# One block of a layer's down-projection: both halves of its tokens for each input block, and a wait for each block

## The reference, cut to what matters

```python
for i in range(4):
    residual = x
    q, k, v = x @ Wq[i] + bq[i], x @ Wk[i] + bk[i], x @ Wv[i] + bv[i]
    Q, K = elu(q) + 1, elu(k) + 1
    KV, Ksum = sum_over_tokens(K * v), sum_over_tokens(K)
    V = Q * KV / (Q * Ksum + 1e-6)
    a = gelu(gelu(V @ Wo[i] + bo[i]))
    x = ln(a + residual, ln1_s[i], ln1_b[i])
    residual = x
    h = gelu(x @ W1[i] + b1[i])          # 128 -> 512
    f = gelu(h @ W2[i] + b2[i])          # 512 -> 128, the down-projection
    x = ln(f + residual, ln2_s[i], ln2_b[i])
x = layernorm(x_in + x)
h = layernorm(gelu(x @ ternary(W_fc).T), ln_w, ln_b)
x = layernorm(x + h @ ternary(W_proj).T)
```

## Time and profile before

| | |
|---|---|
| time before, median of 3 runs | 479.62 us (478.72 to 481.2) |
| time of the profiled execution | 478.65 us |
| its span, first to last instruction | 476.5 us |
| granted TensorE clock, mean over the span | 0.982 |
| PE matmul busy | 442.0 us, 93%, 2074 records |
| DVE busy | 402.6 us, 85%, 1391 |
| ACT busy | 371.9 us, 78%, 483 |
| GpSimd (POOL) busy | 13.9 us, 3%, 19 |

### The profile page before, as it was taken

One profiled execution on the slowest core, in us unless ns is written; L12 is line 12 of the kernel. 1 busy time (PEld: TensorE's weight loads), 2 busy tenths in 40 slices (PEclk: granted clock), 3 DMA queues, 4 the chain that ended last, 5 costly groups with the idle time before them and its releaser, 6 DMA issues.

```text
span 476.5 us, 6527 instructions
## 1 busy us (share of the span) xinstructions
PE 442.0 (93%) x2074; PEld 309.2 (65%) x2074; DVE 402.6 (85%) x1391; ACT 371.9 (78%) x483; POOL 13.9 (3%) x19
## 2 busy tenths in 40 slices
PE   7697999999999999999999999999989999799992
PEld 6465665756575656566656665667566756688992
DVE  5988889995989698969896988698878897978897
ACT  3989877989897989798889888989888717778106
POOL 0000000000000000000000000000000003230000
PEclk9978999999999999999999999999999999999997
DMA  8200000000100000001000000000010102000003
GB/s 285 70 2 0 22 3 0 1 0 1 45 0 2 23 0 1 1 0 45 0 2 1 1 0 1 0 1 2 0 45 12 34 7 82 2 0 23 2 23 132
DMA packets 5360, 10.40 MB, mean 22 GB/s; under 512 B 848, under 2 KB 1872, under 8 KB 5328
## 3 DMA queue, kind: packets, MB, share of 16 engines
q1 hardware_dynamic: 5040, 9.47, 6.1%
q10 hardware_dynamic: 288, 0.52, 0.3%
HBM read 7.90 MB, written 2.10 MB: 21 GB/s over the span
## 4 chain that ended last, share of the span: by engine, by line
PE 41%; DVE 32%; ACT 19%; issue 7%; DMA 1%; ACTq 0%; SPq 0%; DVEq 0%
PE tile L1249 10%; PE tile L1268 7%; PE tile L1226 6%; PE tile L1222 6%; PE tile L1223 5%; DVE stats L770 5%; ACT y L369 3%; DVE y L911 3%; DVE nt L777 2%; ACT y L374 2%; PE tile L1339 2%; PE tile L1328 2%; ACT aa L388 2%; DVE y L880 2%; ACT kq L348 2%
## 5 line engine op out<-in xcount | busy, mean ns | idle before, releaser
L1249 PE MATMUL tile<-h,w 128*128 128x512 f32 x256 | 113.9, 595 | 0.9 <-ACT h L395 0.7
L1222 PE MATMUL tile<-xh,wh 128*128 128x512 f32 x224 | 97.6, 436 | 6.1 <-DVE xh L793 3.4
L1223 PE MATMUL tile<-xh,wl 128*128 128x512 f32 x224 | 89.2, 398 | 0.0
L1249 PEld LDWEIGHTS tile<-h,w 128*128 128x128 f32 x256 | 47.4, 190 | 54.8 <-issue 51.7
L395 ACT ACTIVATE h<-tile,vec 128x1024 f32<-128x1024 f32 x64 | 71.0, 1117 | 13.1 <-PE tile L1226 12.3
L1226 PE MATMUL tile<-xl,wh 128*128 128x512 f32 x224 | 71.1, 398 | 0.7 <-DVE xl L298 0.3
L403 ACT ACTIVATE nt<-tile,work 128x128 f32<-128x128 f32 x140 | 50.7, 482 | 11.3 <-DVE work L739 11.3
L1222 PEld LDWEIGHTS tile<-xh,wh 128*128 128x128 f32 x224 | 42.6, 190 | 24.9 <-DVE xh L793 5.3
L770 DVE BATCH_NORM_STATS2 stats<-tile 128x6 f32<-128x128 f32 x256 | 52.8, 280 | 0.1
L1226 PEld LDWEIGHTS tile<-xl,wh 128*128 128x128 f32 x224 | 41.6, 188 | 13.5 <-DVE xl L799 2.7
L1223 PEld LDWEIGHTS tile<-xh,wl 128*128 128x128 f32 x224 | 42.8, 191 | 9.1 <-issue 2.2
(11 more groups left out here) (173 smaller groups left out, 669.6 us busy)
## 6 DMA issues: line engine op xcount, KB each, us to landing
x<-x_t SPq DMA_DIRECT2D x7, 512.0 KB, 4.1
out_r<-x SPq DMA_DIRECT2D x8, 256.0 KB, 2.0
raw_u<-layers SPq DMA_DIRECT2D x4, 256.0 KB, 3.2
w<-layers SPq DMA_DIRECT2D x4, 256.0 KB, 3.3
raw_a<-layers SPq DMA_DIRECT2D x4, 192.0 KB, 2.8
x<-x_t ACTq DMA_DIRECT2D x2, 256.0 KB, 3.9
wo<-layers SPq DMA_DIRECT2D x4, 64.0 KB, 4.2
fc<-fc_t SPq DMA_DIRECT2D x1, 256.0 KB, 6.5
```

Of the source, the lines that this page charges most:

```text
L1222: pe.matmul(dst, wh[:, w0:w0 + P], xh[:, part(n, p, at)], start=True, stop=False)
L1223: pe.matmul(dst, wl[:, w0:w0 + P], xh[:, part(n, p, at)], start=False, stop=False)
L1249: mm = pe.matmul(dst, w2[:, (t - 1) // 2 % 2, j * P:(j + 1) * P], h[:, p, j * PAIR + at:j * PAIR + at + BANK], start=(j == 0), stop=(j == ...
```

## The change

`down(t, p, half, first)` becomes `down(t, p, j)`, which handles one block for both halves and waits for that block alone. Four calls take the place of two, and they always stand together, at the place where the first of the two calls stood; the calls that stood between the halves come after them.

```diff
-            def down(t, p, half, first):
-                if first:
+            def down(t, p, j):
+                if j == 0:
                     take(slot_of(t, "f", p), (f_ready[p], t))
-                    pe.wait_ge(h_ready[p], FT * t)
                     pe.wait_ge(w2_in[(t - 1) // 2 % 2], 16 * ((t - 1) // 4 + 1))
-                dst, at = halves(slot_of(t, "f", p))[half]
-                for j in range(FT):
+                pe.wait_ge(h_ready[p], FT * (t - 1) + j + 1)
+                for dst, at in halves(slot_of(t, "f", p)):
                     mm = pe.matmul(dst, w2[:, (t - 1) // 2 % 2, j * P:(j + 1) * P], h[:, p, j * PAIR + at:j * PAIR + at + BANK],
                                    start=(j == 0), stop=(j == FT - 1))
-                mm.then_inc(f_mm[p], 1)
+                    if j == FT - 1:
+                        mm.then_inc(f_mm[p], 1)
```

The four places where the order of the calls changes:

```diff
             fold_out(1)
-            down(1, 1, 0, True)
+            down(1, 1, 0)
+            down(1, 1, 1)
+            down(1, 1, 2)
+            down(1, 1, 3)
             attention_out(1, 0)
             back("1", 0, 0, 1)
             back("1", 0, 0, 0)
-            down(1, 1, 1, False)
             attention_out(1, 1)
...
             turned("1", 7, 0)
-            down(7, 0, 0, True)
+            down(7, 0, 0)
+            down(7, 0, 1)
+            down(7, 0, 2)
+            down(7, 0, 3)
             back("1", 7, 1, 0)
             back("1", 7, 1, 1)
-            down(7, 0, 1, False)
             back("1", 7, 0, 1)
...
-            down(8, 0, 0, True)
+            down(8, 0, 0)
+            down(8, 0, 1)
+            down(8, 0, 2)
+            down(8, 0, 3)
             turned("x", 0, 0)
-            down(8, 0, 1, False)
             back("x", 0, 1, 0)
-            down(8, 1, 0, True)
+            down(8, 1, 0)
+            down(8, 1, 1)
+            down(8, 1, 2)
+            down(8, 1, 3)
             back("x", 0, 1, 1)
             back("x", 0, 0, 1)
             back("x", 0, 0, 0)
-            down(8, 1, 1, False)
             turned("2", 8, 0)
```

```diff
             def final_sum(p, u):
                 n, q = p // 2, p % 2
                 dve.wait_ge(x_cb[p], 1)
+                if n == 0:
+                    dve.wait_ge(moment["g"][q], HIDDEN_STEPS)
+                else:
+                    dve.wait_ge(moment["x"][q], 3 * MOMENT_STEPS)
```

More of the change, by code:

```diff
@@ L674, in _, with chain @@
         def _(dve):
-            def norm_work(k, t, p, u=None):
-                pair, rows = home(k, t, p), slice(0, ROWS) if u is None else slice(u * HALF, (u + 1) * HALF)
+            def chain(k, t, p):
+                pair = home(k, t, p)
                 if k == "h":
[L680 to L683, removed]
@@ L685, in moments @@
-            def moments(*norms):
[L690 to L764, removed]
@@ new lines, in mean_square, with variance @@
+            def mean_square(k, t, p):
+                done, base, (rstd, shift, m, v, a, b), width = chain(k, t, p)
+                if k == "g":
+                    dve.wait_ge(done, base)
+                    dve.scalar_tensor_tensor(a, m, -1.0, m, ALU.mult, ALU.mult).then_inc(done, 1)
+                else:
+                    dve.wait_ge(done, base - 2)
+                    dve.scalar_tensor_tensor(a, a, width / 4.0, a, ALU.mult, ALU.mult).then_inc(done, 1)
+            def variance(k, t, p):
+                done, base, (rstd, shift, m, v, a, b), width = chain(k, t, p)
+                dve.wait_ge(done, base + 1)
+                if k == "g":
+                    dve.tensor_tensor(v, a, b, ALU.add).then_inc(done, 1)
+                else:
+                    dve.scalar_tensor_tensor(v, b, width * (BLOCK_EPS if k in "12" else OUTER_EPS), a, ALU.add,
+                                             ALU.add).then_inc(done, 1)
@@ new lines, in guess, with guess_squared @@
+            def guess(k, t, p):
+                done, base, (rstd, shift, m, v, a, b), width = chain(k, t, p)
+                dve.wait_ge(done, base + 2)
+                dve.tensor_scalar(b.bitcast(I32), v.bitcast(I32), -0.5, GUESS, ALU.mult, ALU.add).then_inc(done, 1)
+            def guess_squared(k, t, p):
+                done, base, (rstd, shift, m, v, a, b), width = chain(k, t, p)
+                dve.wait_ge(done, base + 3)
+                dve.tensor_tensor(a, b, b, ALU.mult).then_inc(done, 1)
@@ new lines, in near_one, with quadratics @@
+            def near_one(k, t, p):
+                done, base, (rstd, shift, m, v, a, b), width = chain(k, t, p)
+                dve.wait_ge(done, base + 4)
+                dve.scalar_tensor_tensor(a, a, (LEAD * width ** 0.5) ** 0.25, v, ALU.mult, ALU.mult).then_inc(done, 1)
+            def quadratics(k, t, p):
+                done, base, (rstd, shift, m, v, a, b), width = chain(k, t, p)
+                lead = (LEAD * width ** 0.5) ** 0.25
+                dve.wait_ge(done, base + 5)
+                dve.scalar_tensor_tensor(v, a, Q1 * lead, a, ALU.add, ALU.mult).then_inc(done, 1)
+                dve.scalar_tensor_tensor(shift, a, Q2 * lead, a, ALU.add, ALU.mult).then_inc(done, 1)
@@ new lines, in first_product, with root @@
+            def first_product(k, t, p):
+                done, base, (rstd, shift, m, v, a, b), width = chain(k, t, p)
+                dve.wait_ge(done, base + 6)
+                dve.scalar_tensor_tensor(b, v, C1 * (LEAD * width ** 0.5) ** 0.5, b, ALU.add, ALU.mult).then_inc(done, 1)
+            def root(k, t, p):
+                done, base, (rstd, shift, m, v, a, b), width = chain(k, t, p)
+                dve.wait_ge(done, base + 8)
+                dve.scalar_tensor_tensor(rstd, shift, C2 * (LEAD * width ** 0.5) ** 0.5, b, ALU.add, ALU.mult).then_inc(done, 1)
@@ new lines, in row_shift @@
+            def row_shift(k, t, p):
+                done, base, (rstd, shift, m, v, a, b), width = chain(k, t, p)
+                if k != "g":
+                    dve.wait_ge(done, base + 9)
+                    dve.scalar_tensor_tensor(shift, m, -0.5, rstd, ALU.mult, ALU.mult).then_inc(done, 1)
+            def moments(*norms):
+                for level in (sums, mean_square, variance, guess, guess_squared, near_one, quadratics, first_product, root,
+                              row_shift):
+                    for n in norms:
+                        level(*n)
@@ L1344, in projected, with warm_up @@
                     mm.then_inc(p_mm[p % 2], 1)
-            pe.wait_ge(const_ready, 7)
-            for _ in range(WARM_UP):
-                pe.matmul(tile[3][:, 0:P], ones[:, :], ones[:, :], start=True, stop=True)
+            def warm_up():
+                pe.wait_ge(const_ready, 7)
+                for _ in range(WARM_UP):
+                    pe.matmul(tile[3][:, 0:P], ones[:, :], ones[:, :], start=True, stop=True)
+            warm_up()
             attention_in("k", 0, 0)
```

93 lines of the change are left out of this document (70 added, 23 removed).

## The result

The changed kernel takes 487.93 us (median of 4 runs, 487.23 to 488.24) against 479.17 us before in the same job: ratio 1.0178, 95% interval 1.0162 to 1.0195, 8.8 us slower. Forecast were 488.3 us, in a range of 484.0 to 491.5. The profiled execution took 488.24 us, its span is 486.3; that is 9.8 more than the span of before, one microsecond more than the medians differ by.

What follows compares the result with a forecast made beforehand. No engine alone bounds the kernel; the chain passes between engines, so late starts matter. Profiled 478.65 + 3.44 + 2.25 + 2.2 + 0.8 = 487.35 us, against the median 488.3, range 484.0 to 491.5.

Steps and rivals of the forecast that it cites:

- The wait: Down-projection's finer wait on ACT's gelu: gain 0, at most 0.9 us, since `take` already waits for the last gelu.
- The inner order and the waits: Reordered matmuls: 0, kept -0.6 to +0.6 us; 48 added PE waits: taken as 0, at most 0.08 us each.
- Place A: Step 1, pair 1: `attention_out(1, 0)` and the backs move behind the second half; all engines run 3.44 us late.
- The idle of 2.8 and 1.1 us: Sign at Place A: PE idle for about 2.8 and 1.1 us between 64.6 and 69.4.
- Place B: Step 7: pair 1's two backs move behind the second half, delaying `gelu_down`, `second_sum` and `outer_sum(1)`: +2.25 us.
- Place C: Step 8: pair 1's transposes move behind the second half, delaying `outer_high`, `outer_low` and `second_sum(8, 1)`: +2.2 us.
- pair 0's rows end just in time: At Place C, DVE's statistics and rows for pair 0 end at about 396.3, just before their backs.
- The clock: Granted clock falls after PE's idle: +0.8 us at Place A, 0 at Place C, at most 2.8 each.
- Slack that takes up a place: Rival: unseen slack absorbs delays; two places left 484.1 to 485.3 us, chance 0.08; one 481.8 to 483.0, 0.05.
- The head start of `gelu_down`: Rival: the second half's earlier end decides at the three places, 474.7 us; chance 0.04 together with Loads saved.
- Loads saved: Rival: reused weight blocks aren't reloaded, 128 loads, 24 us, about 464; chance 0.04 with The head start of `gelu_down`.
- No effect: Rival: waits were passed already and the halves' neighbours have slack everywhere, 479.6 us; chance 0.05.

Runs made afterwards that it cites:

- filled: Changed kernel with 9 and 10 matmuls of a constant, result unread, put into PE's idle at Place A and Place C: 488.17 us, ratio 1.0178.
- order_only: Kernel before with old code and waits; only the second halves moved next to the first in the four places: 487.81 us, ratio 1.0186.
- b_alone: Kernel before with only Place B (step 7, pair 0) joined: 480.77 us, ratio 1.0051.
- c_alone: Kernel before with only Place C (step 8, both pairs) joined: 481.90 us, ratio 1.0053.
- coarse_wait: Changed kernel, but block 0 waits for all four activations at once, as before: 488.08 us, ratio 1.0185.
- a_alone: Kernel before with only Place A (step 1, pair 1) joined: 482.87 us, ratio 1.0077.
- b_swapped: Kernel before with Place B joined, and ACT and DVE reordered so the down-projection's gelu and sum come first: 481.05 us, ratio 1.0030.
- c_pair0: Kernel before with only the halves of step 8, pair 0 joined; pair 1 stays divided: 485.58 us, ratio 1.0133.
- pool_earlier: Kernel before with GpSimd adding the constant to pair (0, 0) right after (0, 1), ahead of two shifts: 476.16 us, ratio 0.9931.

## Why the prediction was right, point by point

**The wait gains nothing.** Right: PE waited 0.6 us for ACT's gelu with the fine wait, 0.8 with the coarse one and 0.7 before, and the times agree.

**The inner order and the waits cost nothing.** Right: 0.9997 for the new form without the moves. The widest price that I kept, 0.08 us for a wait, was too high.

**Place A, +3.44.** Right in size: 3.44 without the clock, 3.66 with it, 3.7 by the medians. One step of its story was wrong. I had PE done with `attention_out(1, 1)` as before and idle only from 64.63. In fact the `take` of that product's slot waits for `high` of (0, 0), so it waits 2.17 us itself. The idle of 2.8 and 1.1 us that I named as a sign is therefore 2.17 us ahead of that product and, at full clock, 0.28 and 0.77 behind it (`filled` and `order_only`). The delay is none the worse for it, because PE would have waited for `y` anyway. And the backs had less slack than "out of the way" says: they alone cost 1.8 us by the medians and 2.4 in the trace.

**Place B, +2.25.** Right: 2.24 in the trace, and by the steps that were given; 1.6 to 2.4 in the runs of B alone.

**Place C, +2.2.** Right for `second_sum(8, 1)`: 2.17, and 2.38 at the transposes of the rows where the clock stayed up (`c_alone`). The statement that pair 0's rows end just in time held only because pair 1 was joined too. Alone that move costs 6.3 us.

**The clock, +0.8 at A and 0 at C.** Wrong in both terms, and they cancel in part. At A the fall costs 0.2 us, the difference of 3.66 and 3.44, since PE at full clock waits 0.28 and 0.77 us for DVE there; it fell there in the changed kernel and in `coarse_wait`, and not in `order_only` and `a_alone`. At C it fell in the changed kernel, in `coarse_wait` and in `order_only`, and cost 3.26 - 2.38 = 0.9 us; in `c_alone` it didn't. The sum of the clock terms, 0.8, lies between none and the 1.1 of the changed kernel's trace, so the difference (8.8 us, forecast 8.7) came out by a compensation that I hadn't argued: luck, in a term of 0.8. The rule of the Trainium skill ("TensorE: Matmul & The Clock Gate", "HAM oscillation") held in kind: each fall at A, at C and at the later gap followed an idle gap, with the clock at 0.51 behind those of 2.17 and 2.37 us. Gaps as short as 2.1 us were followed by it in some executions.

**The rivals.** Slack that takes up a place: not seen, the three add up. The head start of `gelu_down`: fell with `b_swapped` and the three single places. Loads saved: fell with the count of loads. No effect: fell with the result.

## What to carry to other kernels

Where a list of work is cut in two and something stands between the parts, look first for who waits for that something: here joining four pairs of halves moved no work off PE and yet cost 8.8 us, and each cost could be read beforehand from a bracket that showed the next engine already idle. What one of the moves costs without its neighbour could not: pair 0 of place C alone cost 6.3 us, where 2 to 3 were expected. A finer wait on an input buys nothing while a coarser wait on the output slot ends last. And a small operation that is slow only at one place of a trace is worth a look at what GpSimd does at that moment.

## What the runs showed of the hardware that was not expected

- VectorE stalled while GpSimd ran: 2.42 us for two operations on 8 columns beside a GpSimd add of 2.40 us, 1.08 beside a shift of 1.13 (both in the kernel before), 2.38 beside an add in the changed kernel, 2.71 instead of 1.22 for an add of two SBUF operands (`c_pair0`). Operations with an operand in PSUM showed no stall: the two of line 930 took 2.36 us beside GpSimd's adds of 4.68 us (`pool_earlier`), no more each than the 1.22 of such an add elsewhere.
- Behind a gap of 2.1 to 2.2 us on TensorE the granted clock fell to the half level (1.2 GHz) in some executions (2.08 in `filled`, 2.17 in `a_alone`) and not in others (2.16 before, 2.20 in `b_alone`); at that level 8 transposes took 1.92 instead of 1.04 us (in `filled`, at 420.6).
- A weight block used twice in succession is loaded twice (192 loads for 192 records), and costs 0.43 us per record in f32 as in any other order.
